# Two-layer graph attention on one core: one column of every third group fetched row by row by SyncE

## The reference

```python
h = (x @ W).reshape(n, heads, -1)
e = leaky_relu(al_s[src] + al_d[dst], 0.2)          # al_s, al_d: scores of h
ex = exp(e - segment_max(e, dst)[dst])
denom = segment_sum(ex, dst)
out = segment_sum(h[src] * (ex / denom[dst])[:, :, None], dst)
```

## Time and profile before

| | before |
|---|---|
| median of three runs | 6099.43 us |
| profiled execution | 6099.06 us, span 6096.9 us |
| DVE busy | 4786.2 us, 79% |
| POOL busy | 3858.2 us, 63% |
| ACT busy | 2743.1 us, 45% |
| DMA packets, bytes | 366,014 packets, 1292.14 MB |

### The profile page before, as it was taken

One profiled execution on the slowest core, in us unless ns is written; L12 is line 12 of the kernel. 1 busy time (PEld: TensorE's weight loads), 2 busy tenths in 40 slices (PEclk: granted clock), 3 DMA queues, 4 the chain that ended last, 5 costly groups with the idle time before them and its releaser, 6 DMA issues. The chain is left out here.

```text
span 6096.9 us, 35661 instructions
## 1 busy us (share of the span) xinstructions
PE 1537.5 (25%) x7221; PEld 1253.2 (21%) x7221; DVE 4786.2 (79%) x9342; ACT 2743.1 (45%) x3115; POOL 3858.2 (63%) x3935
## 2 busy tenths in 40 slices
PE   6777699999600000000000005300000000000000
PEld 4665488888400000000000004200000000000000
DVE  7889677777688888888888876477888877888865
ACT  7886222222144444444444443244444444444430
POOL 1331244444377777777777757777777777777756
PEclk8779799999755555555555557655555555555555
DMA  8999633334366666666666656366666666666659
GB/s 323 338 345 365 240 124 124 122 125 125 103 214 214 214 214 221 219 217 214 214 214 221 218 174 182 103 214 219 219 219 214 214 214 217 221 218 214 213 191 307
DMA packets 366014, 1292.14 MB, mean 212 GB/s; under 512 B 84016, under 2 KB 176240, under 8 KB 329616
## 3 DMA queue, kind: packets, MB, share of 16 engines
q1 hardware_dynamic: 175472, 761.21, 34.2%
q0 software_dynamic: 180320, 476.50, 26.5%
q10 hardware_dynamic: 10048, 52.70, 2.2%
HBM read 681.57 MB, written 608.52 MB: 212 GB/s over the span
## 5 line engine op out<-in xcount | busy, mean ns | idle before, releaser
L169 POOL DMA_INDIRECT rows<-table_d,k_src x3128 | 2978.7, 952 | 953.4 <-issue 953.4
L222 ACT ACTIVATE rows<-totals 128x1088 f32<-128x1088 f32 (+2 forms) x752 | 1651.7, 2196 | 1547.7 <-DVE totals L325 1547.0
L325 DVE TENSOR_TENSOR_SCAN totals<-mask,turned 128x1152 f32<-128x1152 f32 (+2 forms) x752 | 1840.0, 2488 | 0.0
L187 PE MATMUL pB<-diag,k_ones 128*128 128x512 f32 (+1 forms) x4 | 2.9, 821 | 3992.7 <-DVE diag L351 3992.7
L315 DVE TENSOR_TENSOR turned<-rows,pT 128x1088 f32<-128x1088 f32 (+2 forms) x752 | 947.8, 1260 | 0.0
L187 PEld LDWEIGHTS pB<-diag,k_ones 128*128 128x128 f32 x4 | 1.0, 311 | 3993.4 <-DVE diag L351 3993.4
L276 DVE TENSOR_TENSOR z<-rows,ad 128x68 f32<-128x68 f32 (+3 forms) x188 | 38.4, 204 | 616.4 <-DMA rows<-table_d,k_src 616.4
L743 PE MATMUL pH<-hT_pre,w1h 128*128 128x256 f32 x1568 | 460.7, 458 | 120.9 <-ACT hT_pre L621 109.1
L1118 POOL DMA_INDIRECT lone_ea<-in_ea,k_gather x196 | 205.2, 1047 | 424.7 <-DVE mid_feat L1327 350.8
L743 PEld LDWEIGHTS pH<-hT_pre,w1h 128*128 128x128 f32 x1568 | 359.4, 236 | 207.2 <-ACT hT_pre L621 126.8
L687 POOL DMA_INDIRECT dst_rows<-in_dst,full_i x98 | 150.7, 1537 | 337.1 <-DVE full_i L802 309.2
(11 more groups left out here) (249 smaller groups left out, 3655.2 us busy)
## 6 DMA issues: line engine op xcount, KB each, us to landing
sums_d<-rows SPq DMA_DIRECT2D x182, 2244.0 KB, 8.0
ea<-in_ea SPq DMA_DIRECT2D x98, 768.0 KB, 7.3
rows_d<-run SPq DMA_DIRECT2D x97, 768.0 KB, 5.8
pre_d<-pre ACTq DMA_DIRECT2D x49, 1024.0 KB, 6.6
pre_in<-pre_d SPq DMA_DIRECT2D x49, 1024.0 KB, 4.9
rows<-table_d,k_src POOLq DMA_INDIRECT x3128, 2.8
hrow_c<-table_d SPq DMA_DIRECT2D x98, 256.0 KB, 4.4
table_d<-g_rows SPq DMA_DIRECT2D x49, 264.0 KB, 3.0
```

What stands on the lines that cost most here:

```text
L169: p.indirect_dma_start(out=rows[:, g.slot, k, :], out_offset=None, in_=table, in_offset=bass.IndirectOffsetOnAxis(ap=keep["src"][:, e:e + ...
L222: ins = a.activation(rows[:, g.slot, 0:g.size, q * PD:(q + 1) * PD], laid(totals[:, q, :], g.size)[:, :, 1:].rearrange("p d k -> p k d"), ...
L325: v.tensor_tensor_scan(totals[:, q, 0:n], mask[:, g.n % 2, 0:n], turned[q % 2][:, 0:n], 0.0, ALU.mult, ALU.add).then_inc(summed, 1)
```

## The change

In each layer the full groups 4, 7, 10, ... to 88 (29 groups) are now "lone" groups. In these POOL gathers 16 columns, and SP fetches the last one. SP loads the 128 node numbers of the column (`nodes`, from a copy of the indices laid out by column), reads 32 of them at a time into its registers, and issues one DMA of 1,056 bytes for each of the 128 rows, into one of two buffers (`lone`). ACT copies the buffer to the slot (`join`), ahead of its copies of the group before. DVE waits for that copy too before it starts on a lone group. The stores of all groups move from SP to ACT, behind its four copies.

```diff
@@ Group
-        self.landed = 16 * (size + sum(g.size for g in earlier if g.slot == self.slot))
+        self.lone = size == GROUP and self.n >= LONE_FIRST and (self.n - LONE_FIRST) % LONE_EVERY == 0
+        self.lones = sum(g.lone for g in earlier)
+        self.by_pool = size - self.lone
+        self.landed = 16 * (self.by_pool + sum(g.by_pool for g in earlier if g.slot == self.slot))
...
+        lone = sb("lone_", [P, 2, ROW])
+        nodes = sb("nodes_", [1, 2, P], I32)
@@ sync
-            for g in groups:
-                sp.wait_ge(rowed, 2 * g.n + 2)
-                sp.dma_start(outv[:, g.first * ROW:g.end * ROW],
-                             rows[:, g.slot, 0:g.size, :].rearrange("p k w -> p (k w)")).then_inc(stored[g.slot], 16)
+            with_lone = [g for g in groups if g.lone]
+            def load_nodes(j):
+                e = with_lone[j].end - 1
+                sp.dma_start(nodes[0:1, j % 2, :], io["src_cols"][e:e + 1, :]).then_inc(nodes_in[j % 2], 16)
+            load_nodes(0)
+            for j in range(len(with_lone)):
+                if j + 1 < len(with_lone):
+                    load_nodes(j + 1)
+                if j >= 2:
+                    sp.wait_ge(joined, j - 1)
+                sp.wait_ge(nodes_in[j % 2], 16 * (j // 2 + 1))
+                for at in range(0, P, BATCH):
+                    _, found = nc.values_load_multi_w_load_instructions(
+                        nodes[0:1, j % 2, at:at + BATCH], engines=(mybir.EngineType.SP,), min_val=0, max_val=s.NP - 1,
...
+                    for i, node in enumerate(found):
+                        sp.dma_start(lone[at + i:at + i + 1, j % 2, :], table[bass.ds(node, 1), :]).then_inc(lone_in[j % 2], 16)
@@ gpsimd
-                for k in range(g.size):
+                for k in range(g.by_pool):
@@ scalar
+            def join(g):
+                j = g.lones
+                a.wait_ge(stored[g.slot], 16 * g.use)
+                a.wait_ge(summed, PARTS * (g.n - SLOTS + 1) + 1)
+                a.wait_ge(lone_in[j % 2], 16 * P * (j // 2 + 1))
+                a.activation(rows[:, g.slot, g.size - 1, :], lone[:, j % 2, :], ACT.Copy).then_inc(joined, 1)
...
                 if g is not last:
                     spread_mask(groups[g.n + 1])
+                    if groups[g.n + 1].lone:
+                        join(groups[g.n + 1])
...
+                a.wait_ge(rowed, 2 * g.n + 2)
+                a.dma_start(outv[:, g.first * ROW:g.end * ROW],
+                            rows[:, g.slot, 0:g.size, :].rearrange("p k w -> p (k w)")).then_inc(stored[g.slot], 16)
@@ vector, maxima
                 v.wait_ge(gath_in[g.slot], g.landed)
+                if g.lone:
+                    v.wait_ge(joined, g.lones + 1)
```

More of the change, by code:

```diff
@@ L22 @@
 SLOTS = 4
+LONE_FIRST = 4
+LONE_EVERY = 3
+BATCH = 32
 PARTS = 4
@@ L131, in attention @@
         gath_in = [sem(f"gath_in{i}") for i in range(SLOTS)]
+        lone_in = [sem(f"lone_in{i}") for i in range(2)]
+        nodes_in = [sem(f"nodes_in{i}") for i in range(2)]
+        joined = sem("joined")
         stored = [sem(f"stored{i}") for i in range(SLOTS)]
@@ L151, in _ @@
                          first[0:s.EAP, :].rearrange("(p e) h -> p (e h)", p=P)).then_inc(first_in, 16)
-            for g in groups:
-                sp.wait_ge(rowed, 2 * g.n + 2)
-                sp.dma_start(outv[:, g.first * ROW:g.end * ROW],
-                             rows[:, g.slot, 0:g.size, :].rearrange("p k w -> p (k w)")).then_inc(stored[g.slot], 16)
+            with_lone = [g for g in groups if g.lone]
[12 more added lines that the diff above has]
+                        nodes[0:1, j % 2, at:at + BATCH], engines=(mybir.EngineType.SP,), min_val=0, max_val=s.NP - 1,
+                        skip_runtime_bounds_check_because="node numbers below NP; the transfer checks its own bounds")
+                    for i, node in enumerate(found):
+                        sp.dma_start(lone[at + i:at + i + 1, j % 2, :], table[bass.ds(node, 1), :]).then_inc(lone_in[j % 2], 16)
         @block.gpsimd
@@ L1791 @@
                   ea=np.zeros((s.EP, EF), ea.dtype))
+    src_runs = np.zeros(s.EAP, src.dtype)
+    src_runs[:s.E] = src
+    arrays["src_cols"] = np.ascontiguousarray(src_runs.reshape(P, s.EA).T)
     arrays["x"][:s.N] = x
```

## The result

The changed kernel took 6617.75 us (median of five runs, 6580.60 to 6618.42), beside 6099.43 for the kernel before (five runs, 6066.86 to 6103.87): a ratio of 1.0851, interval 1.0815 to 1.0887. It is slower by 8.5%, where 6027 was forecast, and above the range's top of 6580.

What follows compares the result with a forecast made beforehand. POOL's gather list was taken as the bound: 58 lone groups each give back one gather of 1.251 us, 72.6 us, so 6099.06 - 72.6 = 6026.5, beside the likeliest 6027, if SP keeps up; range 6015 to 6580.

Steps and rivals of the forecast that it cites:

- POOL's list and what a gather is worth: In `attention`, POOL's gathers set the pace at 1.251 us each; 58 lone groups each save one, 72.6 us.
- what moves at no cost: On ACT and DVE: store issue (0.34 us), copy from `lone` (about 0.6) and DVE's added wait fit existing gaps.
- the budget: SP's time per column: whole gain up to 64.0 us, no change at 65.5, each us beyond costs 58.
- What SP has to do for one column: SP's work per column: 128 rows 57.6, four register loads 3.6, node numbers 0.45, together 61.7 us.
- rival 1: SP's one-row DMA too slow: at 0.319 us column 69.2, time 6314; at 0.361, 74.6 and 6627; chance 0.24.
- rival 2: SP's register loads slow: at twice 2.1 us each, column 74.85, time 6641; decides from 1.9 us; chance 0.10.
- Rival 3: One DMA engine carries all SP's rows: decides from 0.166 us a row; at 0.20, time 6283; chance 0.08.
- The signs set down: For the DMA queues: SP's rows fast but still landing late would mean one DMA engine carried them all.
- two rules: SP's prices: DMA span includes making descriptors, so column nearer 45 than 62; registers about 200 ns each from HBM, kernel 7152.

Runs made afterwards that it cites:

- one load: Changed kernel with one register load a column instead of four, so three quarters of fetched rows are other nodes'; 6026.77 us, ratio 0.9897 to the kernel before.
- shared column: Changed kernel with ACT fetching 24 of a column's 128 rows, eight in each of three groups, SP 104; 5991.88 us, ratio 0.9853 to the kernel before.
- second store of 8 edges: Changed kernel with a second ACT store behind each group's, of its first 8 edges, to an array nobody reads; 6929.64 us, ratio 1.1368.
- that of one edge: Changed kernel with a second ACT store behind each group's, of one edge, to an array nobody reads; 6576.77 us, ratio 1.0782.
- 8 in each group: Changed kernel with ACT fetching 8 rows in each of three groups, 24 a column, SP 104; 5991.88 us, ratio 0.9853 to the kernel before.
- the one with 10: Changed kernel with ACT fetching 10 rows in each of three groups, 30 a column, SP 98; 5991.83 us, ratio 0.9852.

## Why the prediction was wrong

**Right: POOL's list and what a gather is worth.** The gathers keep their 1.25 us, and where SP keeps up (one load, shared column) the stretches give back 73.6 and 76.8 us; 72.6 was the forecast.

**Right: what moves at no cost.** The stores on ACT alone change nothing; a copy from `lone` takes 0.42 us, 0.6 was assumed.

**Right: the budget.** 64.0 us for a column, 65.5 for no change, 58 us for each us beyond. The columns of 73.44, 74.06, 75.49 and 79.79 us give 460, 497, 579 and 829 by it, and the stretches of the same runs lengthened by 482, 512, 599 and 852: the slope holds, and the point of no change is nearer to 65.2. The column of 63.1 us gave the whole gain, but no run had one between 63.1 and 73.4, so 64.0 itself was not tested.

**Wrong: "What SP has to do for one column", 61.7 us.** It was 74.06, by these terms:

| | forecast | measured |
|---|---|---|
| 128 rows, unheld | 57.6 (0.45 each) | 52.2 (0.408 each) |
| four register loads | 3.6 | 8.5 |
| node numbers, gaps at loads, rest | 0.45 | 1.5 |
| rows held beside a store | none | 11.8 |

The step that failed is that sum: it put rows beside a store at nothing, where the runs show 11.8 us, and it had the register loads at less than half. The row itself came out below the estimate, so rival 1 had nearly the right time (6627 at 74.6 us a column) for a wrong reason: 0.361 us for a DMA where it is 0.225. Register loads were sized as 32 MOVEs, 0.9 us; they take 2.13. That is over the 1.9 us at which rival 2 decides, but with rows of 0.408 it would not have: without the held rows the column is 74.06 - 11.8 = 62.3, within the budget. With loads as forecast and the rows held it is 69.2, 58 x 3.7 = 215 us slower. So by this sum it was the held rows that turned the sign, and the loads that more than doubled the loss. No run took the held rows away by themselves; that the loads alone would not have done it rests on the sum.

A sign of it stood in a row that the prediction quotes for another purpose: the DMAs of L550 take 379 ns in the median and 1591 at most. Ten of the 49 took over 0.6 us. One of them, in the timeline of before, and the queues from 588.6 to 590.3 us (q10 is ACT's, q1 SP's):

```profile
588.68 1.54 SPq L550 DMA_DIRECT2D x_pre<-in_x  x1
...
q10 hardware_dynamic: 72, 0.59, 85.2%
q1 hardware_dynamic: 32, 0.10, 15.1%
```

While ACT's transfer filled most of the engines, SP's DMA took four times its usual time to issue. Beside SP's own transfer, 88.5% of the engines at 74.23 us, a DMA of L577 took its usual 0.33 us, so the row was a reason to put a term in the sum, not a price for it.

Rival 3 had seen that rows and other transfers meet, but priced it by the mean share of the queues, 64.7% from 3000 to 3064 us, as if each row only had to find room. The store isn't spread over the time: it takes 89.9% of all engines for some 6 us, and little of SP's own queue gets through meanwhile. The rows' own packets are not the load. SP's queue and its rows from 1700 to 3700 us in the profile of after:

```profile
q1 hardware_dynamic: 6928, 3.66, 0.9%
...
lone<-table_d SPq DMA_DIRECT2D x3440, 1.0 KB
```

That is about 0.08 us for a row (0.9% x 16 x 2000 us / 3440), about half of the 0.15 that rival 3 took from POOL's packets. All on one engine, a column's rows would fill some 11 of its 74 us (an estimate). The signs set down ("SP's rows are fast and still land late") were not what came; the rows are issued late. The second store of 8 edges shows that the hold grows with the store's bytes, and that of one edge that it doesn't grow with the number of its runs. That the rows meet the store on one DMA engine is argued, not shown: the trace doesn't name the engine of a packet. Why a held row takes about 0.9 us whether the packets are whole or in thirds stays open.

The prediction weighed two rules on these prices. By the Trainium skill's Perfetto Trace Analysis (DMA Instruction, HWDGE) the recorded span holds the making of all descriptors, so fewer of them should shorten it. The trace agrees, 0.225 us for one run beside 0.319 for 128. By the same section of the Trainium skill the span also holds the wait for the descriptor generator, which fits rows of 0.9 us; what a held row waits for, no run shows. By the Trainium skill's Runtime: NRT & Kernel Launch (Instruction fetch mechanics) a load from HBM costs about 200 ns a register; from SBUF these runs show 56 ns and 0.33 us for the load, so that its direction was right against the 0.9 us taken, and its size did not carry over.

## What to carry to other kernels

An engine that only issues DMAs is a resource with a budget of its own: count its address work, register loads and gaps, and set the sum against the time between deadlines, not against its idleness. What its DMAs share with large transfers must be priced while those are in flight, not by a mean share over many microseconds. When such an engine is over its budget by a sixth, as here, moving a fifth of its list into a gap of another queue can be the cure.

## What the runs showed of the hardware that was not expected

- A register load from SBUF beside a store is held for what is left of it: up to 7.1 us in the changed kernel (2.13 otherwise) and 8.1 with the second store of 8 edges.
- ACT's load of 8 numbers takes 0.73 us, its load of 10 takes 2.36 (medians), where 0.056 for each number and 0.33 would give 0.9. It goes by where the ten start in the column's 128 numbers: from number 108 every load takes 1.17 to 1.22 us, from 98 and 118 every one 2.34 to 2.40, while the eights start at 104, 112 and 120. Why, nothing here tells. The line with 8 in each group, and under it the one with 10:

```profile
L159 ACTq TENSOR_LOAD <-nodes x174: 725/730/758, 1643.7 to 5676.1; - x174
```

```profile
L159 ACTq TENSOR_LOAD <-nodes x174: 1168/2359/2401, 1643.9 to 5676.7; - x174
```
